# A masked attention with layer norm on one core: ring of 26 groups, rows of ks in quarters, fewer early bounds of x, the minimum spread by a transpose, the last block's sums in the bank of scores

## The reference

```python
scores = jnp.einsum('nd,md->nm', x, ks)
scores = jax.nn.leaky_relu(scores, negative_slope=0.2)
scores = jnp.where(adj > 0, scores, -9e15)
attn = jax.nn.softmax(scores, axis=1)
y = x + jnp.einsum('nm,md->nd', attn, ks)
out = (y - mean(y)) / jnp.sqrt(var(y) + 1e-5)      # over the 128 columns of each row
```

## Time and profile before

| | us |
|---|---|
| median of three runs | 1570.65 |
| the profiled execution | 1569.98 |
| its span in the trace | 1568.1 |
| TensorE busy | 1511.9 (96%) |
| VectorE busy | 1503.9 (96%) |
| ScalarE busy | 1475.3 (94%) |
| GpSimd busy | 1452.7 (93%) |
| granted TensorE clock, mean share of 2.4 GHz | 0.996 |
| TensorE busy in the first two of 40 slices | 5 and 5 tenths |

### The profile page before, as it was taken

The page is one execution under the profiler, slowest core; times in us unless marked ns, Lnnn a source line. Parts: engine busy times, 40 slices in busy tenths (PEclk is TensorE's granted clock), DMA queues, the critical chain, the costliest instruction groups (busy, mean ns, idle before and its releaser), DMA issues.

```text
span 1568.1 us, 43439 instructions
## 1 busy us (share of the span) xinstructions
PE 1511.9 (96%) x16848; PEld 1421.2 (91%) x16848; DVE 1503.9 (96%) x1809; ACT 1475.3 (94%) x1883; POOL 1452.7 (93%) x1253
## 2 busy tenths in 40 slices
PE   5599999999999999999999999999999999999997
PEld 3389999999999999999999999999999999999996
DVE  7899999999999999999999999999999999999993
ACT  6699999999999999999999999999999999999997
POOL 4799999999999999999999999999999999999998
PEclk9999999999999999999999999999999999999999
DMA  9755666656655556655655655656556655565610
GB/s 368 245 186 182 195 194 191 196 187 193 200 190 189 199 181 197 195 189 190 193 184 193 194 191 185 195 178 196 191 186 194 191 185 191 190 194 186 196 62 8
DMA packets 107134, 296.03 MB, mean 189 GB/s; under 512 B 10801, under 2 KB 40241, under 8 KB 106929
## 3 DMA queue, kind: packets, MB, share of 16 engines
q1 hardware_dynamic: 106928, 293.25, 57.5%
HBM read 289.01 MB, written 4.19 MB: 187 GB/s over the span
## 4 chain that ended last, share of the span: by engine, by line
PE 61%; issue 13%; DVE 10%; ACT 10%; POOL 3%; DMA 2%; DVEq 0%; SPq 0%; ACTq 0%; POOLq 0%
PE weighted L771 17%; PE scores L725 9%; PE scores L727 9%; PE scores L726 9%; PE weighted L787 5%; PE weighted L783 5%; PE weighted L785 5%; ACT ring L468 4%; DVE running L631 4%; DVE ring L647 3%; ACT pt_hi L475 3%; DMA x_probe<-in_x_t 2%; DVE ring L617 2%; POOL pt_lo L376 1%; ACT scores L461 1%
## 5 line engine op out<-in xcount | busy, mean ns | idle before, releaser
L371 POOL TENSOR_TENSOR ring<-ring,floor 128x512 f32<-128x512 f32 (+2 forms) x512 | 714.5, 1396 | 43.2 <-ACT floor L488 43.1
L376 POOL TENSOR_TENSOR pt_lo<-ring,pt_hi 128x512 f16<-128x512 f32 (+1 forms) x512 | 658.9, 1287 | 22.4 <-ACT pt_hi L475 20.0
L617 DVE SCALAR_TENSOR_TENSOR ring<-adj_sb,scores 128x1024 f32<-128x1024 int32 x512 | 622.0, 1215 | 14.6 <-ACT scores L461 14.2
L461 ACT ACTIVATE scores<-scores,shrink 128x1024 f32<-128x1024 f32 x512 | 553.2, 1081 | 49.9 <-PE scores L727 46.1
L468 ACT ACTIVATE ring<-ring,lift 128x1024 f32<-128x1024 f32 x512 | 583.9, 1140 | 5.6 <-POOL ring L371 5.6
L725 PE MATMUL scores<-xt_hi,kt_hi 128*128 128x256 f16 x2048 | 560.2, 274 | 27.9 <-DVE ring L617 23.5
L727 PE MATMUL scores<-xt_hi,kt_lo 128*128 128x256 f16 x2048 | 560.5, 274 | 0.0
L726 PE MATMUL scores<-xt_lo,kt_hi 128*128 128x256 f16 x2048 | 560.2, 274 | 0.0
L631 DVE TENSOR_TENSOR running<-ring,running 128x1024 f32<-128x1024 f32 x448 | 547.3, 1222 | 0.1
L771 PE MATMUL weighted<-k_rows,ring 128*128 128x129 f32 x3584 | 488.4, 276 | 4.2 <-DVE y L668 2.9
L771 PEld LDWEIGHTS weighted<-k_rows,ring 128*128 128x128 f32 x3584 | 441.3, 192 | 16.4 <-ACT ring L468 8.7
(11 more groups left out here) (63 smaller groups left out, 473.1 us busy)
## 6 DMA issues: line engine op xcount, KB each, us to landing
adj_sb<-in_adj SPq DMA_DIRECT2D x512, 512.0 KB, 3.5
ring<-in_ks_t SPq DMA_DIRECT2D x8, 512.0 KB, 7.4
x_row<-in_x SPq DMA_DIRECT2D x32, 128.0 KB, 3.7
out<-normed SPq DMA_DIRECT2D x32, 128.0 KB, 3.6
x_probe<-in_x_t SPq DMA_DIRECT2D x29, 128.0 KB, 3.6
xt_raw<-in_x_t SPq DMA_DIRECT2D x29, 128.0 KB, 4.4
ring<-in_ks SPq DMA_DIRECT2D x12, 128.0 KB, 6.5
k_rows<-in_ks SPq DMA_DIRECT2D x12, 128.0 KB, 3.9
```

Source lines behind the costliest of these rows:

```text
L371: nc.gpsimd.tensor_tensor(here, here, below, ALU.subtract).then_inc(gap_ready, 1)
L376: nc.gpsimd.tensor_tensor(pt_lo[:, g % PARTS, 0:QUAD - whole, :], ring[:, g % RING, whole:, :], pt_hi[:, g % PARTS, 0:QUAD - whole, :], AL ...
L617: nc.vector.scalar_tensor_tensor(ring[:, g % RING, :, :], adj_sb[:, g % ADJS, :, :], 0.0, scores[:, g % 2, :, :], ALU.is_le, ALU.subtract)\
```

## The change

- The ring has 26 places instead of 24, `ks_raw` lies in places 21 to 25, and mask(21) to mask(25) wait for it.
- `ks_raw_loaded` becomes four semaphores; `high_rows(n)` waits for its own quarter, in slots 11 to 14; `part_rows` scales and subtracts quarter by quarter.
- ScalarE takes the last three bounds of ks^T in slots 0 to 2 instead of 1 to 3, its splits move by up to a slot, and the third scale is computed a slot earlier on VectorE and TensorE.
- `X_CUTS` and `probe_slot`: probes in slots 12 to 28 every 4, 34 to 100 every 6, 116 to 270 every 14 (before: 12 to 26 every 2, 30 to 138 every 12, 150 to 290 every 14). A probe's load is issued 4 slots ahead instead of 2. The first two x rows are loaded in slot 20.
- `spread` uses a transpose of the broadcast column instead of a matmul with it.
- In the last 14 groups VectorE subtracts the floor from all four tiles, GpSimd from none.
- In the last block `turn`, `lowest` and `spread` stand two slots later (ScalarE's copy one), and the sums go to the first bank of `scores`, so the first weighing waits for the last mask and not for `finish`.

```diff
     WIDE = QUAD * BLOCK
-    RING = 24
+    RING = 26
     ADJS = 6
...
     CUTS = (0, 1, 4, STEPS)
-    X_CUTS = (0, 3, 11, 21, BLOCKS)
+    X_CUTS = (0, 3, 8, 20, BLOCKS)
...
     AT_FINISH = LAST + AT_WEIGH
+    LEFT_OUT = GROUPS - 2
...
         kt_lo = sb("kt_lo", [P, M], F16)
-        ks_raw = ring[:, 19:24, :, :].rearrange("p g t (a d) -> p (g t a) d", d=D)[:, 0:PARTEDS, :]
+        ks_raw = ring[:, 21:26, :, :].rearrange("p g t (a d) -> p (g t a) d", d=D)[:, 0:PARTEDS, :]
         k_rows = sb("k_rows", [P, WHOLES, LANES + 1], F32)
...
         k_rows_loaded = sem("k_rows_loaded")
-        ks_raw_loaded = sem("ks_raw_loaded")
+        ks_raw_loaded = [sem(f"ks_raw_loaded{n}") for n in range(4)]
         k_rows_ready = sem("k_rows_ready")
...
             x = x_set(b)
-            start, step = ((0, 0), (12, 2), (30, 12), (150, 14))[x]
+            start, step = ((0, 0), (12, 4), (34, 6), (116, 14))[x]
             return start + step * (b - X_CUTS[x])
+
+        def sums(b):
+
+            return weighted if b < BLOCKS - 1 else scores[:, 0, 0:2, :].rearrange("p t n -> p (t n)")
+
+        def late(b):
+
+            return 2 if b == BLOCKS - 1 else 0
+
+        def pool_gaps(g):
+
+            return min(g + 1, ALL - LEFT_OUT)
...
+        def whole_late(s, delay, less=0):
+
+            b = whole(s, delay)
+            if b == BLOCKS - 1 or whole(s - late(BLOCKS - 1) + less, delay) == BLOCKS - 1:
+                return whole(s - late(BLOCKS - 1) + less, delay)
+            return b
+
         def dve_tiles(g):
...
-            return 3 if g >= ALL - GROUPS else min(1 + g % 4, 2)
+            return QUAD if g >= ALL - LEFT_OUT else 3 if g >= ALL - GROUPS else min(1 + g % 4, 2)
...
                 sp.dma_start(ks_raw[:, FIRST_PARTED[j]:FIRST_PARTED[j + 1], :], ks_v[:, j, WHOLE[j]:QUAD, :])\
-                    .then_inc(ks_raw_loaded, 16)
+                    .then_inc(ks_raw_loaded[j // 4], 16)
...
                 load_adj(n)
-            load_x(0)
-            load_x(1)
             for s in SLOTS:
...
                     load_k_rows(2 * (s - 8) + 1)
+                elif s == 20:
+                    load_x(0)
+                    load_x(1)
                 for b in range(X_CUTS[1], BLOCKS):
-                    if s == probe_slot(b) - 2:
+                    if s == probe_slot(b) - 4:
                         load_probe(b)
...
                 pool.wait_ge(scale_step, scales_there(2))
-                pool.wait_ge(k_hi_ready, 4)
-                low = k_parts[:, :, LOW:LOW + D]
-                high = k_parts[:, :, HIGH:HIGH + D]
-                nc.gpsimd.tensor_scalar(ks_raw, ks_raw, scale_rows, 1.0, ALU.mult, ALU.mult).then_inc(k_scaled_ready, 1)
-                pool.wait_ge(k_scaled_ready, 1)
-                nc.gpsimd.tensor_tensor(low, ks_raw, high, ALU.subtract).then_inc(k_lo_ready, 1)
+                for n in range(4):
+                    rows = slice(n * PARTEDS // 4, (n + 1) * PARTEDS // 4)
+                    pool.wait_ge(k_hi_ready, n + 1)
+                    nc.gpsimd.tensor_scalar(ks_raw[:, rows, :], ks_raw[:, rows, :], scale_rows, 1.0, ALU.mult, ALU.mult)\
+                        .then_inc(k_scaled_ready, 1)
+                    pool.wait_ge(k_scaled_ready, n + 1)
+                    nc.gpsimd.tensor_tensor(k_parts[:, rows, LOW:LOW + D], ks_raw[:, rows, :],
+                                            k_parts[:, rows, HIGH:HIGH + D], ALU.subtract).then_inc(k_lo_ready, 1)
                 pool.wait_ge(k_rows_loaded, 16 * GROUPS)
...
                 g = group(s, AT_GAP)
-                if g is not None:
+                if g is not None and dve_tiles(g) < QUAD:
                     gap(g)
...
             def exponentials(g):
-                act.wait_ge(gap_ready, g + 1)
+                act.wait_ge(gap_ready, pool_gaps(g))
                 act.wait_ge(dve_gap_ready, g + 1)
...
             def high_rows(n):
-                act.wait_ge(ks_raw_loaded, 16 * GROUPS)
+                act.wait_ge(ks_raw_loaded[n], 16 * 4)
                 act.wait_ge(scale_step, scales_there(2))
...
                     bend(g)
-                if s == 0:
-                    split_ks_t(2)
-                if s < 5:
-                    split_ks_t(s + 3)
-                if 1 <= s < 4:
-                    bound_ks_t(s + 4, s + 2)
-                if 5 <= s < 13:
+                if s < 3:
+                    split_ks_t(s + 2)
+                if s < 3:
+                    bound_ks_t(s + 5, s + 3)
+                if s == 3:
+                    split_ks_t(5)
+                if 3 <= s < 13:
                     split_ks_t(s + 3)
...
                     split_x(1)
-                if 12 <= s < 16:
-                    high_rows(s - 12)
+                if 11 <= s < 15:
+                    high_rows(s - 11)
                 for b in range(X_CUTS[1], BLOCKS):
...
                         bound_x(b)
-                b = whole(s, AT_SPREAD)
+                b = whole_late(s, AT_SPREAD, 1)
                 if b is not None:
...
                 wait(dve, weighted_ready, g + 1 - RING)
-                if 19 <= g < 24:
-                    dve.wait_ge(k_lo_ready, 1)
+                if 21 <= g < 26:
+                    dve.wait_ge(k_lo_ready, 4)
                 if g == 8:
...
                 at = b % 2
-                total = weighted[:, 0:SIDES * LANES].rearrange("p (j w) -> p j w", j=SIDES)
+                total = sums(b)[:, 0:SIDES * LANES].rearrange("p (j w) -> p j w", j=SIDES)
                 dve.wait_ge(weighted_ready, GROUPS * (b + 1))
...
                     split_ks_t(2)
-                if s == 4:
+                if s == 3:
                     dve.wait_ge(mag_k_bounded, 6)
...
                     magnitude(mag[:, K_ALL:K_ALL + 1], mag_k[:, :])
-                if s == 5:
+                if s == 4:
                     most(2)
...
                         magnitude(mag[:, X_SETS[x]:X_SETS[x] + 1], mag_x[:, X_CUTS[x]:X_CUTS[x + 1]])
-                b = whole(s, AT_LOWEST)
+                b = whole_late(s, AT_LOWEST)
                 if b is not None:
...
                 for j in range(SIDES):
-                    last = nc.tensor.matmul(floors[:, b % 2, j * P:(j + 1) * P],
-                                            low[:, b % 2, j:j + 1].to_broadcast([P, P]), eye[:, :],
-                                            start=True, stop=True)
+                    last = nc.tensor.transpose(floors[:, b % 2, j * P:(j + 1) * P],
+                                               low[:, b % 2, j:j + 1].to_broadcast([P, P]), eye[:, :])
                 last.then_inc(spread_ready, 1)
...
                 pe.wait_ge(prob_ready, g + 1)
-                if q == 0:
+                to = sums(b)
+                if q == 0 and b < BLOCKS - 1:
                     wait(pe, y_ready, SIDES * b)
+                elif q == 0:
+                    pe.wait_ge(masked_ready, ALL)
                 if g == 0:
                     pe.wait_ge(k_rows_ready, 1)
-                    pe.wait_ge(k_lo_ready, 1)
+                    pe.wait_ge(k_lo_ready, 4)
                 for t in range(WHOLE[q]):
                     for j in range(SIDES):
-                        nc.tensor.matmul(weighted[:, j * LANES:(j + 1) * LANES],
+                        nc.tensor.matmul(to[:, j * LANES:(j + 1) * LANES],
                                          ring[:, g % RING, t, j * P:(j + 1) * P], k_rows[:, FIRST_WHOLE[q] + t, 0:LANES],
...
                         at = j * LANES
-                        nc.tensor.matmul(weighted[:, at:at + LANES], pt_hi[:, g % PARTS, t, cols], high,
+                        nc.tensor.matmul(to[:, at:at + LANES], pt_hi[:, g % PARTS, t, cols], high,
                                          start=False, stop=False, skip_group_check=True)
-                        nc.tensor.matmul(weighted[:, at:at + D], pt_hi[:, g % PARTS, t, cols], low,
+                        nc.tensor.matmul(to[:, at:at + D], pt_hi[:, g % PARTS, t, cols], low,
                                          start=False, stop=False, skip_group_check=True)
-                        last = nc.tensor.matmul(weighted[:, at:at + LANES], pt_lo[:, g % PARTS, t, cols], high,
+                        last = nc.tensor.matmul(to[:, at:at + LANES], pt_lo[:, g % PARTS, t, cols], high,
                                                 start=False, stop=done, skip_group_check=True)
...
             for s in SLOTS:
-                if s == 6:
+                if s == 5:
                     magnitudes(2, bank)
...
                     magnitudes(1, bank)
-                b = whole(s, AT_TURN)
+                b = whole_late(s, AT_TURN)
                 if b is not None:
...
                         magnitudes(x_stage(b + 2), running[:, 2, :])
-                b = whole(s, AT_SPREAD)
+                b = whole_late(s, AT_SPREAD)
                 if b is not None:
...
                 g = group(s, AT_WEIGH)
```

## The result

| | before | after |
|---|---|---|
| median of the runs, taken together | 1570.12 (1568.99 to 1571.44) | 1553.39 (1552.35 to 1553.48) |
| the profiled execution / its span | 1569.98 / 1568.1 | 1553.36 / 1551.6 |
| TensorE, VectorE busy | 1511.9, 1503.9 | 1502.5, 1502.6 |
| ScalarE, GpSimd busy | 1475.3, 1452.7 | 1475.7, 1440.9 |

The ratio is 0.9892 with a 95% interval of 0.9874 to 0.9909: faster, 16.7 us by the medians. The forecast was 1552.6, so the time is off by 0.8 us. The gain is off by more, 16.7 against the 18.1 forecast, because the median of before, now of four runs, is 1570.12 and not 1570.65. The terms are off by more still, in both directions. The 16.5 us between the two spans divide at two marks, the first weighing (the start of the first matmuls into `weighted`) and the last mask (VectorE's last `mask`, group 511).

A forecast was written before the change was run, and what follows sets the result against it. TensorE was taken to bound the long middle, VectorE close behind, and GpSimd the tail. Gains 6.3 + 6.9 + 3.0 + 1.9 = 18.1 us took 1569.98 to 1551.9; the median, 0.67 above, gave 1552.6, range 1547 to 1562.

The forecast's parts named there:

- Spread: Saturated middle: the transpose makes the floor's spread 0.22 us a block shorter, 6.3 us in 30 blocks.
- Rival A: Middle: the spread's transposes cost their full duration, 0.56 us, 0.11 more than now; 1562.2 us in all, chance 0.07.
- D: Spread: the fp32 transpose of a broadcast column runs far slower than a dense one; whole kernel slower, e.g. 1579, chance 0.03.
- Fill: Start of the kernel: ks rows in quarters, a slot earlier, bring the first floor subtraction from 73.71 to 66.8, 6.9 us.
- coming free: In the fill: GpSimd is done with the last low half of ks^T at 47.8 instead of 48.36.
- upper bound of 9.2: Fill's largest gain, if quarters cost only a quarter of 12.7 us each and VectorE's `least` finds a gap.
- Probes: Bounding of x: loads issued four slots ahead gain 3.0 us, between 0 and 5.6, with 2.6 us of loss left.
- Tail: End of the kernel: VectorE's fourth tile, late floor and sums in the scores' bank gain 1.9 us, between -1.5 and 3.9.
- ScalarE fills this with exp(495); exp(500) half a microsecond earlier: In the tail: ScalarE works through the floor's delay, so exp(500) comes half a microsecond earlier than before.
- Ring: 26 places instead of 24 gain nothing, except the place of ks_raw counted in the fill.
- Rival B: Middle: VectorE or ScalarE becomes the bound, so the spread gives 3 us and the probes 0; 1558.8, chance 0.15.
- Rival C: Fill: VectorE's two-operand `least` or ScalarE's fuller slots hold mask(21) back, gaining 3 instead of 6.9; 1556.5, chance 0.15.

The follow-up runs named there:

- e1_matmul: The changed kernel with the floor spread by the fp32 matmul again instead of the transpose; 1559.43 us.
- e10_high12: The changed kernel with the four high quarters of ks back in slots 12 to 15 instead of 11 to 14; 1552.61 us.
- e12_best: The changed kernel with high quarters in slots 12 to 15, k_rows scaled on ScalarE, VectorE subtracting all from group 494, last block not late; 1549.77 us.
- e5_before_lead4: The kernel before with probe loads issued four slots ahead instead of two, for blocks bound at slot 30 and later; 1564.56 us.
- e11_ring24: The changed kernel with a ring of 24 places again and ks_raw in places 19 to 23; 1553.64 us.

## Why the prediction was right, and where its terms were not

**Spread: 6.3, measured 6.4 in the middle, by e1_matmul 6.2 there and 5.8 in the medians.** Right, with its mechanism. Rival A is out: two transposes of a broadcast column hold TensorE 0.22 us in the chain. D is out by the same row. The Trainium skill's 275 ns for a PE-mode transpose ("TensorE: Matmul & The Clock Gate", Part 4) agrees with the 281 ns of the earlier trace rows as a duration; what a stream of them costs is the distance.

**Fill: 6.9, measured 4.7.** The quarters cost 14.3 us against 14.8 forecast, k_rows 4.25 against 4.2. The step that failed is "coming free": 47.8 forecast, 49.66 measured, 1.9 us late. It has three parts. Half a microsecond is the slot: I moved the high quarters a slot earlier on GpSimd's side of the sum but did not follow them on ScalarE's queue, where the first one (44.80, 1.24 us) now stands ahead of the last split of ks^T (46.94), for which GpSimd's last low half waits; e10_high12 and e12_best, without it, show the old distance. Another 0.8 is that the slots before it run later: mask(12) starts at 47.17 instead of 46.33, and at 46.90 to 48.77 in the ten variants made from the change, against 45.48 and 46.13 in the two made from before. The last 0.6 is what I took off 48.36, half a microsecond of it for the earlier third scale: that gain is not there. Why these slots are later, no run took apart. (The upper bound of 9.2 comes to 9.0 by its own terms.) So GpSimd's subtraction and mask(21) gained 5.5 us each, where 6.9 and 6.7 to 8.0 were forecast. The last 0.8 is a thing the sum did not have: from mask(21) to the first weighing it is 2.60 us before and 3.43 in the change, where TensorE had the lower clock (last section).

**Probes: 3.0, measured 4.7.** The bounds held it (5.6). I kept 2.6 us of loss for the denser probes; nothing of the kind was left, since e5_before_lead4 shows that the waits were for the load and not for ScalarE's time. The prediction named both the longer lead and the room on ScalarE, and gave the wrong one the weight.

**Tail: 1.9, measured 0.5.** The later floor was forecast (2 us), and came (2.06). What failed is "ScalarE fills this with exp(495); exp(500) half a microsecond earlier": it is 1.0 later. The sum counted ScalarE's own work after the floor and no wait for TensorE; measured, ScalarE waits 0.86 and 0.35 us for the weighing, in and behind the stretch at half clock. In e10_high12, with the same tail, the full clock and no such wait, exp(500) starts 19.71 us after the last mask (19.99 before) and the last denominator 44.71 (46.45 before): 1.7 us gained, near the forecast. So the count holds where TensorE keeps its clock, and the term at nothing was TensorE. That the clock makes the wait is argued from six traces that agree, not from an edit. From exp(500) on, 1.4 us were gained as said.

The terms miss by -2.2 (fill), +1.7 (probes) and -1.4 (tail): that the time is within 0.8 is partly luck.

**Ring: 0,** right (e11_ring24). **Rival B** (VectorE the bound) did not decide but is near: 0.07 us a block. **Rival C** came half true: mask(21) is 1.2 us or more short of its forecast, but no two-operand `least` held it as before (1.98 us instead of 5.23).

**What the terms don't say.** They don't add. Transpose alone 2.9, lead alone 5.6, together with the old kernel's rest they would be 8.5; in the change undoing the one costs 5.8 and the other 13.2. By the table above a microsecond that ScalarE waits for a probe costs 0.6 us with the old spread and 0.8 with the new one, so the longer lead is worth more in the new kernel, and the transpose more with the longer lead. That is not all of the 13.2: with the new slots and the short lead ScalarE also waits longer, 14.3 us instead of 8.0. The old kernel with both edits together was not run, so how much is the slots and how much the spread stays open.

## What to carry to other kernels

When the engine that bounds is made faster, read the slack of the next one first: waiting elsewhere that cost little starts to cost more, so remove those waits in the same step. How far ahead a small load must be issued is read from the waits of the engine that needs it: here two slots were too few, and four left no wait. When a piece is moved a slot earlier, write down the whole queue of the engine that makes it, since what it overtakes may be what the other engine waits for. And before a microsecond between two variants is explained, compare the granted clock of the same stretch in both.
